# Two attentions with heads of 8 rewritten as one slot program, and a residual bias moved from TensorE to GpSimd

## What is computed

```python
sim = jnp.einsum('bhid,bhjd->bhij', q, k) * SCALE
attn = jax.nn.softmax(sim, axis=-1)
out = jnp.einsum('bhij,bhjd->bhid', attn, v)
return out.transpose(0, 2, 1, 3).reshape(B, Nq, INNER_DIM) @ Wo + bo
```

## Time and profile before

| | |
|---|---|
| median of 3 runs | 6537.66 us (6531.66 to 6538.91) |
| the profiled execution | 6532.18 us, its span 6530.4 us |
| self attention of layer 0 | from 23.1 to 339.2 us in the span |
| feed-forward of layer 0 | mostly 680 to 2640 us (drains until some 2715) |
| cross attention of layer 1 | from 2959.7 to 3249.8 us |
| attention of layer 3 | from 5283 us to some 5750 |

### The profile page before, as it was taken

How to read it: one execution, slowest core, us unless ns; L and a number is a source line. 1 busy time by engine, 2 the same in 40 slices (tenths; PEclk the granted TensorE clock), 3 DMA queues, 4 the chain that set the end, 5 groups by cost and what they waited for, 6 DMA issues and landing times. The chain is left out here.

```text
span 6530.4 us, 86354 instructions
## 1 busy us (share of the span) xinstructions
PE 4875.4 (75%) x27785; PEld 2919.0 (45%) x27787; DVE 4377.8 (67%) x8424; ACT 2893.0 (44%) x4778; POOL 2359.2 (36%) x2096
## 2 busy tenths in 40 slices
PE   6645799999999999676642467666687779953667
PEld 4534466666666666334421122222366344422434
DVE  4522788888888888474435699999754335638635
ACT  2211477777777776462211354454223324532311
POOL 0011666666666666251011366666300220000100
PEclk8755899999999999787665799999898868975878
DMA  0000100000000000000000000000000000002000
GB/s 13 0 4 0 32 1 14 5 14 5 9 10 7 13 4 1 4 0 2 2 0 0 7 0 0 1 0 0 12 0 12 0 15 4 5 11 54 6 21 6
DMA packets 73573, 48.58 MB, mean 7 GB/s; under 512 B 27696, under 2 KB 67785, under 8 KB 72457
## 3 DMA queue, kind: packets, MB, share of 16 engines
q1 hardware_dynamic: 71177, 43.12, 2.6%
q0 software_dynamic: 2048, 1.05, 0.1%
HBM read 39.53 MB, written 1.18 MB: 6 GB/s over the span
## 5 line engine op out<-in xcount | busy, mean ns | idle before, releaser
L2962 POOL TENSOR_TENSOR l_attn_read<-l_attn_state,l_attn_c_rows 128x1024 f32<-128x1024 f32 x256 | 603.6, 2358 | 329.4 <-DVE l_attn_state L2865 328.5
L1848 POOL TENSOR_TENSOR l_ffn_t<-l_ffn_t 128x512 f32<-128x512 f32 x384 | 488.3, 1272 | 595.2 <-DVE l_ffn_t L1716 595.2
L203 POOL TENSOR_SCALAR rstd<-mean_var 128x4 f32<-128x4 f32 (+1 forms) x36 | 8.3, 231 | 1622.7 <-DVE mean_var L192 1622.7
L2865 DVE TENSOR_TENSOR_SCAN l_attn_state<-l_attn_decay,psum 128x1024 f32<-128x1024 f32 x256 | 584.9, 2285 | 8.0
L1448 PE MATMUL psum<-l_ffn_wq,l_ffn_xsT 128*128 128x512 f32 x1152 | 564.9, 599 | 20.5 <-DVE l_ffn_t L1716 12.0
L2667 PE MATMUL psum<-l_attn_read,ident 128*128 128x512 f32 x1024 | 495.4, 606 | 5.4 <-DVE l_attn_yz L2873 3.0
L2658 PE MATMUL psum<-l_attn_parts,pick 96*128 96x512 bf16 x512 | 200.9, 395 | 308.4 <-DVE psum L2857 308.2
L1859 POOL TENSOR_TENSOR l_ffn_p<-l_ffn_p,l_ffn_sm 128x512 f32<-128x512 f32 x384 | 399.2, 1040 | 63.7 <-DVE l_ffn_sm L1748 46.8
L1854 POOL TENSOR_TENSOR l_ffn_t<-l_ffn_t,l_ffn_ss 128x512 f32<-128x512 f32 x384 | 400.4, 1043 | 0.7 <-DVE l_ffn_ss L1731 0.7
L2784 ACT COPY l_attn_c_rows<-psum 128x512 f32<-128x512 f32 x256 | 149.6, 584 | 469.0 <-PE psum L2658 468.8
L1613 ACT COPY l_ffn_pT<-psum 128x512 f32<-128x512 f32 x384 | 224.4, 584 | 272.4 <-PE psum L1478 268.8
(11 more groups left out here) (762 smaller groups left out, 12108.9 us busy)
## 6 DMA issues: line engine op xcount, KB each, us to landing
l_ffn_wq<-in_L_ffn_Wqkv SPq DMA_DIRECT2D x6, 1536.0 KB, 6.1
l_xattn_toep<-s4d_taps SPq DMA_DIRECT2D x4, 2048.0 KB, 17.1
l_ffn_wo<-in_L_ffn_Wo SPq DMA_DIRECT2D x6, 512.0 KB, 7.7
l_ffn_w<-in_L_ffn_W SPq DMA_DIRECT2D x6, 341.0 KB
l_ffn_w<-in_L_ffn_w SPq DMA_DIRECT2D x3, 512.0 KB, 5.6
l_attn_k<-l_attn_dense_k POOLq DMA_DIRECT2D x64, 16.0 KB, 1.8
l_attn_q<-l_attn_dense_q SPq DMA_DIRECT2D x64, 16.0 KB
l_xattn_conv_y<-l_xattn_conv_rows SPq DMA_DIRECT2D x64, 16.0 KB, 2.2
```

The lines of the kernel that those rows point to most:

```text
L1848: nc.gpsimd.tensor_tensor(t1[:, m % G, i, :], t1[:, m % G, i, :], t2[:, x % 3, :], ALU.add).then_inc(added, 1)
L2865: nc.vector.tensor_tensor_scan(state[:, k % 3, :], decay[:, k % 3, :, :, :].rearrange("p h g t -> p (h g t)"), drive, 0.0, ALU.mult, ALU.a ...
L2962: nc.gpsimd.tensor_tensor(read[:, k % 3, :].rearrange("p (h n) -> p h n", h=2), state[:, k % 3, :].rearrange("p (h n) -> p h n", h=2), row ...
```

## The change

`small_heads(K, pre, local)` replaces both attentions: `local` is true for layer 0 (mask, chunk term) and false for layer 1 (120 keys, bias). It has no loop and one `stage` for all four groups. Every engine walks through the same slots `t`, 16 to a group (`PER`), and does what `a_at`, `b_at`, `o_at` and `misc_at` say of the slot.

A unit is now one head of all four batches. Head `4j + s` lies in the range `j` of 32 partitions of the tile of set `s`. Slot by slot PE makes, for two units at once (two ranges), the scores with queries on the partitions (`score`, "A"), from which DVE takes only the maximum (`peak`); PE transposes the negated maxima of a set (`mt`) into an extra row of the queries (`q9`); then it makes the same scores again with keys on the partitions (`turned_score`, "B"), already less the maximum, and ACT's exponential writes `pT` straight from PSUM (`exp`). `value` ("O") multiplies four units of a set. A has banks 0 and 1, B 2 and 3, O 4, and the single items share banks 5 to 7 in turn. Of 16 slots of a group, counted from 6, A stands in slots 6 to 13, B in 11 to 18, O in 14, 16, 18 and 20; the next group's slots begin 16 later, so its A stands beside the last items of the group before. The residual is added by a matmul with the identity (`fin`), and the layer norm is applied by ACT out of the same bank (`apply`).

In the feed-forward block the four matmuls of one row are gone; POOL adds `b2`, now loaded to all 128 partitions, to the residual beforehand (`add_b2`).

The diff, cut to its core:

```diff
-def l0_attn(K):
+def small_heads(K, pre, local):
...
+    dh, SETS, ROW, PER, CS = 8, 4, 32, 16, 64
+    NK = T if local else NC_
+    KEYS = G * NK
...
+        q4, k4 = sb("q4", [128, 2, SETS, GT]), sb("k4", [128, SETS, KEYS])
+        q9 = sb("q9", [128, SETS, GT])
+        v = sb("v", [128, 2, G, H16, ROW])
+        top = sb("top", [128, G, SETS, 128])
+        pT = sb("pT", [128, 8, GT])
+        oT = sb("oT_sum", [128, 2, GT])
+        inv = sb("inv", [128, 2, G, 4])
...
+        O = K.bank[4]
+        spare = [K.bank[5 + i] for i in range(3)]
+
+        def a_at(t):
+            g, u = divmod(t - 6, PER)
+            return [(g, u // 2, 2 * (u % 2) + i) for i in range(2)] if 0 <= g < NG and u < 8 else []
+
+        def b_at(t):
+            g, u = divmod(t - 11, PER)
+            return [(g, u // 2, 2 * (u % 2) + i) for i in range(2)] if 0 <= g < NG and u < 8 else []
+
+        def o_at(t):
+            done = b_at(t - 2)
+            return done[1][:2] if done and done[1][2] == 3 else None
+
+        OFFSETS = [("x", -4), ("q", -2), ("v", 1), ("k", 3), ("mt", 9, 0), ("mt", 11, 1), ("mt", 13, 2), ("mt", 15, 3), ("ot", 16, 0), ("ot", 18, 1),
+                   ("ot", 20, 2), ("ot", 22, 3), ("o2", 24), ("fin", 26)] + ([("cr", 7), ("vm", 21)] if local else [])
+
+        def misc_at(t):
+            for name, at, *s in OFFSETS:
+                g, u = divmod(t - at, PER)
+                if u == 0 and 0 <= g < NG:
+                    return (name, g, *s)
+
+        slots = range(-4, NG * PER + 16)
+        use = {key: n for n, key in enumerate(misc_at(t) for t in slots if misc_at(t) is not None)}
+        index = lambda g, s, j: 16 * g + 4 * s + j
+        acc_of = lambda g, s: 4 * g + s
+        ON_ACT = ("x", "k", "cr", "o2")
...
+                def score(keys):
+                    g, s, j0 = keys[0]
+                    for key in keys:
+                        n = index(*key)
+                        if n >= 2:
+                            pe.wait_ge(maxed, n - 1)
+                    if s == j0 == 0:
+                        wait_moved(pe, "q", g)
+                        wait_moved(pe, "k", g)
+                        if local and g == 0:
+                            pe.wait_ge(masks, 1)
+                    if local:
+                        for j in (j0, j0 + 1):
+                            nc.tensor.matmul(K.bank[j % 2], K.ident16[:], rows(mask16[:], G), start=True, stop=False, skip_group_check=True)
+                    for b in range(G):
+                        for j in (j0, j0 + 1):
+                            r = slice(ROW * j, ROW * j + ROW)
+                            last = nc.tensor.matmul(K.bank[j % 2][:, b * NK:b * NK + NK], q4[r, g % 2, s, b * T:b * T + T], k4[r, s, b * NK:b * NK + NK],
+                                                    start=not local, stop=True, skip_group_check=local)
+                            if b == G - 1:
+                                last.then_inc(a_done, 1)
+
+                def turned_score(keys):
+                    g, s, j0 = keys[0]
+                    for key in keys:
+                        n = index(*key)
+                        if n >= 2:
+                            pe.wait_ge(exped, n - 1)
+                    if j0 == 0:
+                        wait_moved(pe, "mt", g, s)
+                    if local:
+                        for j in (j0, j0 + 1):
+                            nc.tensor.matmul(K.bank[2 + j % 2], K.ident16[:], rows(mask_t16[:], G), start=True, stop=False, skip_group_check=True)
+                    for b in range(G):
+                        for j in (j0, j0 + 1):
+                            r = slice(ROW * j, ROW * j + ROW)
+                            last = nc.tensor.matmul(K.bank[2 + j % 2][:NK, b * T:b * T + T], k4[r, s, b * NK:b * NK + NK], q9[r, s, b * T:b * T + T],
+                                                    start=not local, stop=True, skip_group_check=local)
+                            if b == G - 1:
+                                last.then_inc(b_done, 1)
+
+                def value(g, s):
+                    acc = acc_of(g, s)
+                    pe.wait_ge(exped, 4 * acc + 4)
+                    if acc >= 1:
+                        pe.wait_ge(o_moved, acc)
+                    for b in range(G):
+                        at = slice(b * T, b * T + T)
+                        for j in range(4):
+                            last = nc.tensor.matmul(O[ROW * j:ROW * j + ROW, at], v[:NK, g % 2, b, 4 * j + s, :], pT[:NK, (4 * acc + j) % 8, at],
+                                                    start=True, stop=True, skip_group_check=True)
+                    last.then_inc(o_done, 1)
+
...
+                def other(key):
+                    n, kind, g = use[key], key[0], key[1]
+                    ps = bank_of(key)
+                    if n >= 3:
+                        pe.wait_ge(moved[n % 3], n // 3)
...
+                    if kind == "o2":
+                        for s in range(SETS):
+                            wait_moved(pe, "ot", g, s)
+                        if local:
+                            wait_moved(pe, "vm", g)
+                            for b in range(G):
+                                nc.tensor.matmul(ps[:, b * T:b * T + T], o[:, b, :], K.ident[:], start=True, stop=False)
+                                last = nc.tensor.matmul(ps[:, b * T:b * T + T], term[:, b, :], K.ident[:], start=False, stop=True)
+                        else:
+                            last = turn(ps, lambda b: o[:, b, :])
+                    if kind == "fin":
+                        wait_moved(pe, "o2", g)
+                        nc.tensor.matmul(ps, K.ident[:], K.x_all[:, g * G:(g + 1) * G, :], start=True, stop=False, skip_group_check=True)
+                        if not local:
+                            nc.tensor.matmul(ps, K.ones[0:1, :], rows(bo[:], G), start=False, stop=False, skip_group_check=True)
+                        for b in range(G):
+                            last = nc.tensor.matmul(ps[:, b * D:b * D + D], o_turned[:, b * T:b * T + T], wo[:], start=False, stop=True,
+                                                    skip_group_check=True)
+                    last.then_inc(filled, 1)
...
+                for t in slots:
+                    if a_at(t):
+                        score(a_at(t))
+                    if b_at(t):
+                        turned_score(b_at(t))
+                    if o_at(t) is not None:
+                        value(*o_at(t))
+                    if misc_at(t) is not None:
+                        other(misc_at(t))
...
+                def exp(key):
+                    n = index(*key)
+                    act.wait_ge(b_done, n + 1)
+                    if n >= 8:
+                        act.wait_ge(o_done, (n - 8) // 4 + 1)
+                    nc.scalar.activation(pT[:NK, n % 8, :], K.bank[2 + n % 2][:NK, :], ACT.Exp, scale=scale).then_inc(exped, 1)
...
+                    if kind == "k":
+                        if g:
+                            act.wait_ge(b_done, 16 * g)
+                        else:
+                            act.wait_ge(inited, 1)
+                        for s in range(SETS):
+                            ins = nc.scalar.activation(k4[:, s, :], ps[:, :KEYS], ACT.Identity, scale=own[:, s:s + 1], bias=minus[:, s:s + 1])
+                        if local:
+                            if g:
+                                act.wait_ge(kmean_made, g)
+                            ins = nc.scalar.copy(k_dense[:].rearrange("p b t -> p (b t)"), ps)
...
+                def apply(g):
+                    key = ("fin", g)
+                    act.wait_ge(rstd_ready, g + 1)
+                    for b in range(G):
+                        ins = nc.scalar.activation(K.x_all[:, g * G + b, :], bank_of(key)[:, b * D:b * D + D], ACT.Identity, scale=rs[:, b:b + 1], bias=nb[:, b:b + 1])
+                    ins.then_inc(moved[use[key] % 3], 1)
+
+                for t in slots:
+                    before, done = misc_at(t - 1), misc_at(t - 3)
+                    if before is not None and before[0] in ON_ACT:
+                        evacuate(before)
+                    for key in b_at(t):
+                        exp(key)
+                    if o_at(t) is not None:
+                        move_sum(*o_at(t))
+                    if done is not None and done[0] == "fin":
+                        apply(done[1])
...
+                def peak(key):
+                    g, s, j = key
+                    n = index(*key)
+                    dve.wait_ge(a_done, n + 1)
+                    if g:
+                        wait_filled(dve, "mt", g - 1, s)
+                    ps = K.bank[n % 2][:, :KEYS].rearrange("p (b k) -> p b k", b=G)
+                    nc.vector.reduce_max(top[:, :, s, ROW * j + dh * ((s + 1) % SETS)], ps, AX).then_inc(maxed, 1)
...
+                    if kind == "mt":
+                        s = key[2]
```

(21 more changed lines are left out.)

350 lines of the change are left out of this document (200 added, 150 removed).

## The result

| | before | after |
|---|---|---|
| median of 4 runs | 6535.65 us (6531.66 to 6538.91) | 6364.52 us (6361.44 to 6367.65) |
| ratio after / before | | 0.9738, 95% interval 0.9722 to 0.9755 |
| layer 0's attention, in the span | 316 us | 252.6 us |
| layer 1's cross attention | 287 us | 236 us |
| between the two | 2622.4 us | 2564.0 us |

171 us less, where 190 were forecast: 6364.5 against 6348. The two attentions are measured from the first load of their weights to the end of their last layer norm, what lies between them from the first load after layer 0 (340.10 before, 277.47 after) to the cross attention's first load (2962.48, 2841.49). So layer 0 gave 63 us (forecast 67), the feed-forward block 58 (55), the cross attention 51 (68). Unrounded that is 173 us; the spans of the two profiled executions differ by 168, since the rest of the program took some 5 us longer in the second.

The account below looks back on a forecast made before the run. PE's busy time was taken to bound the feed-forward block, and waits between small stages to add to it in the attentions. Layer 0 67, cross attention 68 and feed-forward 55 us sum to 190 us less: 6348 us, range 6270 to 6450.

Parts of the forecast that it names:

- The bias of the feed-forward block: Feed-forward block: removing the one-row matmuls from 96 batches of w2 makes it 55 us shorter.
- Rival 4: Feed-forward block: the bias gives half or less because POOL's add makes DVE or PE wait; 6375 to 6400 us, chance 0.10.
- The A pair's wait, 0.84 to 0.87: Both attentions: an A pair waits 0.84 to 0.87 us for both maxima of the pair before, as shown by layer 3.
- The sign that was named for it: A pairs 2.4 us apart in layer 0 at 1.00; prediction wrong if further apart than 2.9 us at 1.00.
- Layer 0: 249 us: Layer 0's attention: 14 us to the first A, groups of 61, 52, 52 and 64; 249 against 316, 67 us less.
- The wait for the layer norm: Both attentions, groups 2 to 4: PE waits 3.1 us for the bank of fin, and the clock falls some 4 us.
- The wait for the keys: Both attentions: the first A waits for ACT to move the keys, 0.9 us in layer 0, 1.4 in the cross attention.
- The cross attention: 222 us: Layer 1's cross attention: 17 + 47 + 2 x 46.5 + 58.5 + 7 for clock dips; 222 against 290, 68 us less.
- Rival 3: Both attentions: the low clock holds, with pairs in two ranges; 6519 us, with lighter forms from 6430 on, chance 0.15.
- Borders of shape: Both attentions: each change of shape between mask and score costs 0.1 us, 16 in a group, 6 us in layer 0.
- Rival 5: Both attentions: low clock, and each border of shape around the 128 pairs drains the array; slower, up to 6596 us, chance 0.05.
- Rival 2: Both attentions: higher clock nearly throughout; layer 0 99 us less, cross attention 104, 6277 us in all, chance 0.12.

Follow-up runs that it names:

- e1: Kernel before with only the feed-forward block's part of the change (bias added on POOL, no one-row matmuls): 6479.3 us.
- e2: Kernel before with the one-row bias matmul of w2 replaced by one over all 128 rows with as many columns: 6497.3 us.
- e3: Changed kernel with POOL's 24 bias adds replaced by an instruction of 128 x 1 elements giving the same signal: 6365.75 us.
- e7: Changed kernel with both bank changes, those of e5 and e6: 6322.4 us.
- e9: e7 with the keys made two slots earlier, in two buffers, and the value projection two slots later: 6276.85 us.
- e5: Changed kernel with the A pairs of slots 7 and 9 in the two banks that B uses later: 6312.0 us.
- e6: Changed kernel with another rotation of the three spare banks, so nobody needs the bank of fin before slot 15: 6355.0 us.
- e10: e5 with the keys made two slots earlier and the value projection two slots later: 6303.25 us.
- e11: e9 with unread matmuls before the first A pair, four in layer 0 and three in the cross attention: 6261.4 us.
- e4: Changed kernel without layer 0's mask matmuls, and with the same matmuls with a mask of zeros in the cross attention: 6408.8 us, one run.
- e8: Changed kernel with the cross attention's o2 made as in layer 0, eight matmuls (half with zeros) instead of four transposes: 6366.2 us.

## Why the prediction was right, and where it was off

- **What bounds the kernel.** Right: PE's busy time in layer 0 is the same, and what came off are its waits (100 to 38 us).
- **The bias of the feed-forward block: 55 us.** Right: 56 in e1, 58 between the two attentions; a batch at 0.67 us for 0.70. The split of the price was right too, 0.38 us for the borders (0.35 in the forecast) by e2. POOL's add was priced at 1.04, from a multiplication instead of the add in L1848, and takes 1.27 us, which costs nothing (e3); the 1 us allowed for it was not needed. Rival 4 falls.
- **The A pair's wait, 0.84 to 0.87.** Wrong, and the code would have told: layer 3 has three banks for A, so a pair asks for one maximum of the pair before; here are two, and it asks for both. It is 0.6 us more, near the 0.69 of one maximum. The first group of layer 0 took 67.3 us for 61, the later ones 55.2 and 56.8 for 52, by this wait and by dips of the clock of 6.8 and 3.4 us where one of 4 was counted. The sign that was named for it, A pairs 2.4 us apart and none beyond 2.9 at the higher clock, speaks against the prediction: they are 3.15 us apart, with a turn in between, and by that sign this term was wrong.
- **Layer 0: 249 us.** 11.4 to the first A (forecast 14), 67.3, 55.2, 56.8 and 62.0 (64 with the tail): 252.6 in all. The 4 us by which it missed are a difference: the first A came 2.6 us early, and the groups took 6 us more than their 235. Mean clock 0.82 for 0.85, PE busy 85% of it.
- **The wait for the layer norm, 3.1 us in groups 2 to 4.** It is there, 2.56 us, released by ACT's layer norm and with the dip of the clock behind it. It comes in groups 2 and 3 only: in the last group no x item follows, so the rotation no longer lands on the bank of `fin`. The wait for the keys is 0.95 as forecast, 1.26 for 1.4 in the cross attention.
- **The cross attention: 222 us.** This is the step that failed: "in the cross attention A alone may lose it too (6 us a group in all)". Measured are 11.5 us to the first A, 49.1, 54.7, 54.7 and 66.5, where 17, 47, 46.5, 46.5 and 58.5 stood. In a group of 54.7 us the clock is down for 37.6 us, not for a few. The runs say why: each wait ahead of or between A pairs can let it fall, and then it stays down until the value item and q, eight slots later, or longer (e7); 6 us were priced as if it came back at once. In e9, where the clock is up from 2860.3 to 2955.9 and the waits are short, a group takes 34.7 us. Rival 3's mechanism took this half of the program in part. The groups took 225 us where 205.5 were forecast with their dips, and it is luck that the first A came 5.5 us early and hid part of it. These parts make 18 of the 19 us missing in the sum: 17 here, 4 in layer 0, and 3 the other way in the feed-forward block.
- **Borders of shape** between mask and score at 0.1 us: 0.53 at the higher clock for two masks and the border, as taken. Rival 5 falls; its rule holds for the one row (e2), but the pairs of 32 rows follow masks and transposes at 1.09 and 2.01 us as priced.
- **Rival 2**, 6277 us with the clock up nearly throughout, is the time of e9, but only in part for its reason. Layer 0 is at 1.00 from 81.8 us on, yet the first group is not, the cross attention has a mean clock of 0.79, and e9 is without waits that rival 2 had in its sum. That the numbers meet is luck.

That waits let the clock fall, and that their removal can give back more than their length, is shown by e5 (43 us for 10.6 in the cross attention), e6 (15 for 5 in layer 0) and e9 (46 for 7). That it need not is shown by e6 in the cross attention (nothing for 5) and by e10 against e5 (9 for 7); when it does was not settled. That the clock rises behind the value item and q is seen in groups 1 to 3 of both programs of after and in the first group of layer 0 in e9 and e11; but in e7 it did not, and no run tells what it takes. Value items without q left it down for 19 us in the last group of the cross attention (3045.89 to 3065.6). Why layer 0 holds the clock better than the cross attention (0.82 in the changed kernel, against 0.63 in e4's with its masks of zeros) stays open: the pairs there are of 120 keys and `o2` is shorter, and e8 gave only part of it.

## What to carry to other kernels

Price a wait on TensorE by where it stands: one of 1.3 us among matmuls that use part of the rows can halve the clock of the next 20 to 40 us, so look in the windows for stretches with PE nearly full at 0.50 and remove the wait ahead of them, by another bank, an earlier producer or, where it can't go, matmuls that nobody reads. When a wait's length is taken from other code, compare the number of buffers in the two waits first. A one-row matmul for a bias costs more than its columns (0.38 us a time on top of them here; taking 96 of them out saved 56 us in all): add the bias on an engine that has time. And price that add from a row of the same operation.

## What the runs showed of the hardware

- TensorE stayed at 1.2 GHz for 41.0 us with PE busy for 40.57 (e7), and for 47.6 us with 45.92 busy (e9), most of it pairs of 32 rows with transposes and, in e9, masks. A mix with the same pairs, but with value items and projections in each group, held 2.4 GHz for 160 us (e9, e11). The Trainium skill (TensorE: Matmul & The Clock Gate, HAM oscillation — how this bites in real kernels) has a wait that throttles TensorE so that what follows starts cold. Its waits are of some 3 to 5 us; here the clock fell behind waits of 1.26 to 2.56 us, though not behind each (e5, e9), and it then stayed down for up to 51 us under nearly full load.
- Matmuls over all rows whose result is thrown away, 3.6 us of them in a wait of 3.4, shortened layer 0 by 10 us (e11).
- One kernel's runs lie up to 39 us apart, the longest with the lowest mean clock (e5: 6307.6 to 6347.0, 0.861 against 0.856); with three kinds of waits gone five runs lay within 7.5 us (e9).
- A matmul of one row between matmuls of 128 costs 0.38 us beyond its columns for the two changes (e2); one of 85 rows costs nothing beyond them (0.22 us for two records).
